# The lower part of the mixed filters, subtracted by VectorE in place of GpSimd

## The reference, cut to what matters

```python
x = x + attention(_gn(x))          # 1x1 projections, softmax of q over channels, of k over pixels, RMS norms
g = _gn(x)
r = sigmoid(relu(fc @ relu(rconv @ pooled(g)) + fc_b))   # (b, 3, c_in): a gate for each expert and input channel
w = einsum('bkc,kocij->bocij', r, expert_weight)         # filters of each image, 3 x 3 x 128 x 128
x = x + conv3x3(g, w)                                    # padding 1, stride 1
```

## Time and profile before

| | us |
|---|---|
| median of 3 runs (426.83 to 427.61) | 427.45 |
| the profiled execution | 427.47 |
| its span, first to last instruction | 425.8 |

### The profile page before, as it was taken

One profiled execution on the slowest core, in us unless ns is written; L12 is line 12 of the kernel. 1 busy time (PEld: TensorE's weight loads), 2 busy tenths in 40 slices (PEclk: granted clock), 3 DMA queues, 4 the chain that ended last, 5 costly groups with the idle time before them and its releaser, 6 DMA issues.

```text
span 425.8 us, 8949 instructions
## 1 busy us (share of the span) xinstructions
PE 410.8 (96%) x2575; PEld 360.0 (85%) x2575; DVE 345.7 (81%) x779; ACT 304.2 (71%) x942; POOL 265.7 (62%) x212
## 2 busy tenths in 40 slices
PE   7999989999999999999999999999999999999996
PEld 6889888879897888889898989889898989787785
DVE  4377989898988989897989899898989796978720
ACT  1688877888696777868686877879686868654321
POOL 4745859585774858577684848485876857543220
PEclk9899999999999999999999999999999999999999
DMA  6520261425324262606262444426062623405232
GB/s 202 231 101 2 99 237 62 180 84 187 147 98 153 96 248 94 240 36 228 100 247 100 165 179 145 200 75 239 35 242 99 247 100 117 181 12 237 99 149 99
DMA packets 19076, 61.63 MB, mean 145 GB/s; under 512 B 3024, under 2 KB 4320, under 8 KB 19040
## 3 DMA queue, kind: packets, MB, share of 16 engines
q1 hardware_dynamic: 19040, 61.21, 38.1%
HBM read 19.29 MB, written 8.39 MB: 65 GB/s over the span
## 4 chain that ended last, share of the span: by engine, by line
PE 54%; DVE 19%; issue 12%; ACT 10%; POOL 2%; DMA 1%; DVEq 1%; ACTq 0%; POOLq 0%
PE ps_conv L2176 19%; PE ps_y L2108 6%; PE ps_att L2076 6%; ACT y_scaled L820 4%; ACT expert_raw L847 4%; PE ps_y L2114 3%; DVE w_full L1523 3%; PE ps_y L2098 3%; PE ps_qkv L2057 3%; DVE y_scaled L1409 3%; PE ps_qkv L2059 2%; PE ps_qkv L2058 2%; DVE q_max L1337 2%; PE ps_att L2090 1%; DVE w_second L1516 1%
## 5 line engine op out<-in xcount | busy, mean ns | idle before, releaser
L2176 PE MATMUL ps_conv<-left,w_hi 128*128 128x512 f32 (+2 forms) x192 | 63.4, 398 | 0.0
L2176 PE MATMUL ps_conv<-right,w_hi 128*128 128x512 f32 (+2 forms) x192 | 62.9, 391 | 0.0
L761 ACT ACTIVATE qk<-ps_qkv,scale 128x256 f32<-128x256 f32 x128 | 54.7, 469 | 10.7 <-PE ps_qkv L2059 6.6
L589 POOL TENSOR_TENSOR w_lo<-w_full,w_hi 128x1152 fp32r<-128x1152 f32 x16 | 54.5, 3404 | 6.1 <-ACT w_hi L853 4.5
L596 POOL TENSOR_TENSOR left<-zeros 128x64 fp32r<-128x64 f32 x16 | 5.0, 313 | 77.9 <-DMA right<-img_lo 77.9
L570 POOL TENSOR_TENSOR scale<-ssq,minus_half 128x8 f32<-128x8 f32 x16 | 31.1, 1941 | 20.9 <-DVE ssq L1402 20.9
L544 POOL TENSOR_TENSOR x_lo<-x,x_hi 128x1024 fp32r<-128x1024 f32 x16 | 38.6, 2414 | 5.5 <-ACT x_hi L751 5.5
L2057 PE MATMUL ps_qkv<-wqk_hi,x_hi 128*128 128x256 f32 x128 | 40.5, 317 | 1.2 <-ACT qk L761 1.2
L2176 PEld LDWEIGHTS ps_conv<-right,w_hi 128*128 128x128 f32 x192 | 36.1, 188 | 5.9
L853 ACT ACTIVATE w_hi<-w_full 128x1152 fp32r<-128x1152 f32 x16 | 18.7, 1168 | 30.3 <-DVE w_full L1529 30.1
L2176 PEld LDWEIGHTS ps_conv<-left,w_hi 128*128 128x128 f32 x192 | 35.4, 189 | 5.0
(11 more groups left out here) (166 smaller groups left out, 1240.0 us busy)
## 6 DMA issues: line engine op xcount, KB each, us to landing
xa<-in_x_dram SPq DMA_DIRECT2D x16, 512.0 KB, 3.8
xb<-in_x_dram SPq DMA_DIRECT2D x16, 512.0 KB, 4.6
left<-img_hi SPq DMA_DIRECT2D x16, 511.5 KB, 2.9
right<-img_hi SPq DMA_DIRECT2D x16, 511.5 KB, 3.7
left<-img_lo SPq DMA_DIRECT2D x16, 511.5 KB, 2.9
right<-img_lo SPq DMA_DIRECT2D x16, 511.5 KB, 3.7
out_dram<-expert_raw SPq DMA_DIRECT2D x15, 512.0 KB, 3.0
expert_raw<-_conv_expert_weight_dram SPq DMA_DIRECT2D x1, 1728.0 KB, 9.4
```

The costliest lines, as they stand in the source:

```text
L589: nc.gpsimd.tensor_tensor(w_lo[p][:, :, :].rearrange("p t o -> p (t o)"), w_full[:, :], w_hi[p][:, :, :].bitcast(F32).rearrange("p t o -> ...
L761: nc.scalar.activation(qk[:, t, :], ps_qkv[t % 2][:, 0:QK], ACT.Copy, scale=scale1[:, t:t + 1]).then_inc(qkv_done, 1)
L2176: last = mm(into, weight[:, tap, :], pixels[:, top + down:bottom + down, :], start=(n == 0 and part == 0), stop=(n == TAPS - 1 and part == 2))
```

## The change

`filters_low` leaves GpSimd's list and joins VectorE's, with the same operands, the same waits and the same semaphore. In the loop it stands right behind `q_subtract`, on the filters that the step before has summed. In the lists by hand it stands behind `q_subtract` too, for images 0 to 13. That of image 14 stands behind `gn2_aggregate(15)`, and that of image 15 at the very end. On SyncE the last two calls are exchanged: the store of image 14 comes ahead of the store of image 15.

```diff
@@ sync, last_steps
                 store(13, 1)
+                store(14, 0)
                 store(15, 1)
-                store(14, 0)
@@ gpsimd
-            def filters_low(b, p):
-                pool.wait_ge(w_full_done, b + 1)
-                ...
@@ gpsimd, step (and likewise in first_steps and last_steps, for every image)
                 do(image_edges, t, p, 5)
-                do(filters_low, t, p, 5)
                 do(low1, t, p, 2)
@@ vector
+            def filters_low(b, p):
+                dve.wait_ge(w_full_done, b + 1)
+                dve.wait_ge(w_hi_done, b + 1)
+                if past(b, 2):
+                    dve.wait_ge(conv_ps, 2 * (b - 1))
+                v.tensor_tensor(w_lo[p][:, :, :].rearrange("p t o -> p (t o)"), w_full[:, :],
+                                        w_hi[p][:, :, :].bitcast(F32).rearrange("p t o -> p (t o)"),
+                                        ALU.subtract).then_inc(w_lo_done, 1)
@@ vector, step
                 do(q_subtract, t, p, 2)
+                do(filters_low, t, p, 4)
                 do(k_maximum, t, p, 2)
@@ vector, first_steps
                 q_subtract(2, 0)
+                filters_low(0, 0)
                 k_maximum(2, 0)
...
                 q_subtract(4, 0)
+                filters_low(2, 0)
                 k_maximum_all(4, 0)
@@ vector, last_steps
                 q_subtract(15, 1)
+                filters_low(13, 1)
                 k_maximum(15, 1)
...
                 gn2_aggregate(15, 1)
+                filters_low(14, 0)
                 gn2_pool(15, 1)
...
                 filters_centre(15, 1)
+                filters_low(15, 1)
```

More of the change, by code:

```diff
@@ L639, in first_steps @@
                 image_edges(0, 0)
-                filters_low(0, 0)
                 low1(3, 1)
@@ L650, in first_steps @@
                 image_edges(1, 1)
-                filters_low(1, 1)
                 low1(4, 0)
@@ L661, in first_steps @@
                 rms2(3, 1)
-                filters_low(2, 0)
                 low1(5, 1)
@@ L672, in first_steps @@
                 rms2(4, 0)
-                filters_low(3, 1)
                 low1(6, 0)
@@ L685, in last_steps @@
                 image_edges(11, 1)
-                filters_low(11, 1)
                 low1(14, 0)
@@ L696, in last_steps @@
                 image_edges(12, 0)
-                filters_low(12, 0)
                 low1(15, 1)
@@ L705, in last_steps @@
                 image_edges(13, 1)
-                filters_low(13, 1)
                 q_normalise(15, 1)
@@ L711, in last_steps @@
                 image_edges(14, 0)
-                filters_low(14, 0)
                 routing_products(15, 1)
@@ L715, in last_steps @@
                 image_edges(15, 1)
-                filters_low(15, 1)
             first_steps()
@@ L1707, in first_steps @@
                 q_subtract(3, 1)
+                filters_low(1, 1)
                 k_maximum(3, 1)
@@ L1787, in first_steps @@
                 q_subtract(5, 1)
+                filters_low(3, 1)
                 k_maximum(5, 1)
@@ L1829, in last_steps @@
                 q_subtract(13, 1)
+                filters_low(11, 1)
                 k_maximum(13, 1)
@@ L1867, in last_steps @@
                 q_subtract(14, 0)
+                filters_low(12, 0)
                 k_maximum(14, 0)
```

## The result

The changed kernel takes 465.52 us (median of 3 runs, 462.4 to 467.03), against 427.45 before. The ratio is 1.0883, with an interval of 1.0843 to 1.0922. The forecast was 444.6 us, in a range of 438.5 to 448.5: the sign was right and the size was not. The time grew by 38.1 us, and I had counted 17.1. The profiled execution took 465.52 us with a span of 463.8 us, so the traces differ by 38.0 us. One run of experiment e9 (452.4 us) was in a slower state of the chip and is left out of its row; all other times are of fast runs.

A forecast was written before the change was run, and what follows sets the result against it. TensorE was taken as the bound, with 0.06 us of slack per step. Steps 16.2, tail +2.4 and stores -1.5 summed to 17.1 us on 427.5, giving 444.6 us, in a range of 438.5 to 448.5.

The forecast's parts named there:

- The subtraction leaves GpSimd: On GpSimd, x_lo and q's normalisation can come up to 3.5 us earlier; counted as nothing.
- rival C: VectorE's other instructions shorten without a busy GpSimd, or part of the shift is caught up: 439.2 us, chance 0.12.
- The exception: Fourteenth filter's step, where y_scaled waited 1.09 us for GpSimd's scale and the convolution for w_lo: -0.2 us.
- The subtraction's time: Moved subtraction on VectorE: 1.36 us long, blocking the queue for 1.28 us, bounds 1.14 and 1.42.
- The step without the hold: Each loop step grows by 1.28 us to 24.7, as TensorE waits at L2070 and L2114; 16.2 us over all steps.
- The tail: Image 14's filters, behind image 15's aggregation on VectorE, come late; TensorE stands for 2.7 us: +2.4 us.
- The stores: At the end, image 14's store goes out earlier, ahead of image 15's: -1.5 us, between -0.4 and -1.7.
- Rival B: Not slower: VectorE's idle time swallows the subtraction and steps cost nothing; 428.2 us, chance 0.05.
- Rival D: Dearer steps: TensorE's pauses lower its granted clock, or the subtraction costs over 1.42 us; about 451 us, chance 0.08.
- The quoted rule on engine selection: Two-input elementwise work belongs on VectorE, GpSimd being about two times slower; set against 3.50 and 1.36 us.

The follow-up runs named there:

- e9: e8 without the wait that holds x_lo on GpSimd until q_exp is done; 445.5 us.
- e1: The changed kernel with one more wait on GpSimd: x_lo starts only when w_lo on VectorE is done; 447.0 us.
- e2: The kernel before with low1 (x_lo) moved ahead of filters_low in GpSimd's list, nothing else; 483.9 us.
- e4: The kernel before with the last two stores on SyncE exchanged, nothing else; 425.3 us.
- e8: Changed kernel, w_lo's products last, subtractions 0 to 13 ahead of gn1_stats, 14 behind y_scaled(15), x_lo waiting for q_exp; 430.2 us.

## Why the prediction was wrong, and where it was right

**The step that failed** is the first one, "The subtraction leaves GpSimd": "Both can now come up to 3.5 us earlier. I count nothing for that: the chain of the step goes through neither". What was put at nothing measured 18.5 us (465.5 against e1's 447.0). The chain doesn't go through x_lo in the kernel before, that is true. But x_lo moved from a place where none of VectorE's instructions is held to the start of k_max_part and q_exp. Its old place, timelines of GpSimd and VectorE, kernel before:

```profile
233.84 2.40 POOL L544 TENSOR_TENSOR x_lo<-x,x_hi 128x1024 fp32r<-128x1024 f32 x1
...
234.02 1.21 DVE L1352 TENSOR_REDUCE q_sum<-q_exp 128x32 f32<-128x1024 f32 x1
...
235.56 1.28 DVE L1421 SCALAR_TENSOR_TENSOR x<-ps_y,g_c,xb 128x1024 f32<-128x1024 f32 x1
```

The subtraction on GpSimd had been a shield. It waited behind q_exp itself (part of its 3.50 us, where an idle VectorE leaves 2.69), and it kept x_lo away until q_exp was over. e1 makes x_lo wait again and gives 447.0. e2 takes the shield away with nothing moved to VectorE and costs 56 us, with q_exp held too.

**The reading behind it** failed in rival C: "the contention falls on GpSimd alone". I took it from w_second, 1.42 us beside GpSimd's idle time and 1.42 at 224.98. But at 224.98 GpSimd was idle as well: it ran nothing between 224.36 and 229.03. A comparison of two undisturbed cases showed nothing. The trace of before held the counterexample, in the one step where the order slipped. VectorE and GpSimd, kernel before:

```profile
134.09 0.35 DVE L1308 TENSOR_TENSOR k_max_part<-k_quarter 128x128 f32<-128x128 f32 x1
134.37 1.31 DVE L1344 TENSOR_TENSOR q_exp<-qk,q_max 128x1024 f32<-128x1024 f32 x1
...
134.00 0.31 POOL L596 TENSOR_TENSOR left<-zeros 128x64 fp32r<-128x64 f32 x1 [7.95 <-DMA right<-img_lo]
134.25 0.36 POOL L597 TENSOR_TENSOR right<-zeros 128x64 fp32r<-128x64 f32 x1
134.56 2.62 POOL L570 TENSOR_TENSOR scale<-ssq,minus_half 128x8 f32<-128x8 f32 x1
```

k_max_part 0.35 and q_exp 1.31 us, against 0.28 or 0.29 and 1.21 to 1.23 in all other steps: small, because the edges that GpSimd was running had 64 columns and took 0.31 us. Behind a reader of 2.40 us it could be 2 us, an estimate from these rows. The scale behind them was held in its turn, 2.62 in place of 1.64 us. Read so, the rows give mechanism and size: up to 2 us in each step in which x_lo comes ahead of k_max_part.

**The exception** was wrong by sign: the step of y_scaled(4) was to become 0.2 us shorter, and became 1.6 longer. The same hold acts from the other side here. VectorE and GpSimd after:

```profile
143.28 0.28 DVE L1289 TENSOR_TENSOR k_max_part<-k_quarter 128x128 f32<-128x128 f32 x1
143.48 1.22 DVE L1325 TENSOR_TENSOR q_exp<-qk,q_max 128x1024 f32<-128x1024 f32 x1
144.62 1.35 DVE L1511 TENSOR_TENSOR w_lo<-w_full,w_hi 128x1152 fp32r<-128x1152 f32 x1
...
148.00 1.22 DVE L1390 TENSOR_TENSOR y_scaled<-ps_y,scale 128x1024 f32<-128x1024 f32 x1 [1.58 <-POOL scale L570]
...
143.27 2.86 POOL L587 TENSOR_TENSOR left<-zeros 128x64 fp32r<-128x64 f32 x1 [8.04 <-DMA right<-img_lo]
```

The edges on GpSimd, 0.31 us of work, came beside three instructions of VectorE with two inputs and ended at 146.13, just behind the last of them. So the engines don't take strict turns: VectorE's three went through back to back, each in its own time, although the edges' start is recorded 0.01 us ahead of the first. The scale, queued behind them, was late, and y_scaled waited 1.58 us for it.

**Right, by the runs.** The subtraction's time: forecast 1.36, measured 1.36, and 1.27 us between the starts of w_lo and of k_max (305.29 to 306.56), forecast 1.28. The step without the hold: forecast 24.7, measured 24.6 in e1 and 24.55 here. The tail: forecast a wait of 2.7 and +2.4, measured 2.37 at convolution 14 and a tail 0.5 us longer (35.5 against 35.03 from y_scaled(15)), for a forecast of 2.4 - 1.5. Against e4, which has the stores alone, the tail is 1.8 us longer. The stores: -1.5 forecast, -1.4 to -2.0 measured.

**Rival B**, that VectorE's idle time swallows the work, was rightly small at this place. e8 shows what was true in it: elsewhere in the list the same work costs 0.68 us a step in place of 1.2, and that much only with route_zr held. **Rival D** was small but real: the clock fell to about half in three windows of together 10 us. By the steps compared above that cost about 3 us (an estimate).

The quoted rule on engine selection (the Trainium skill, GPSIMD Engine Reference, Engine selection) gives the engine's time rightly. The fair pair is 1.36 against 2.69 us, twice as long; the 3.50 that I set against it has a hold in it. The rule says nothing about the place. The Trainium skill's Key points on the same page have the contention; I read them as a gain for VectorE only.

## What to carry to other kernels

When work leaves an engine, list what moves up in its queue and lay each such instruction beside the other engine's timeline at its new time, also where the chain passes through neither. For VectorE and GpSimd this means every pair of a two-input instruction on VectorE and a reader on GpSimd, since one of the two can wait for the whole of the other. Place work by the waits of its engine and not by its busy share: the same 1.27 us cost 1.2 us a step ahead of y_scaled, 1.1 behind it, and 0.7 where VectorE waits for a transfer, with a small instruction held in that 0.7.

## What the hardware showed that I had not expected

The hold is whole, not a slowdown: 0.28 us became 2.15 beside a 2.35 us reader, and q_exp became 3.67 in e2. It falls on either engine: GpSimd's rstd of 2 columns took 1.81 us in place of 0.70 in e8 where VectorE's w_lo was ahead of it.

It caught instructions with one tensor as input too. route_zr (0.86 against 0.17 us) and gate_n (0.79 against 0.23) scale three columns and were held beside GpSimd's x, while a reduction with one input ran through beside x_lo in 0.42 us. The Trainium skill (SBUF — State Buffer, Who interferes with whom) names such scalings as instructions that can enter a mode using the shared ports, and reductions as none. The runs agree with it on both, though no run here varied the operands to show that it is the mode.

TensorE's clock fell from 2.4 to 1.2 GHz (granted clock 0.50) for about 3 us at 69 us, behind two pauses of 2.10 and 1.39 us, and again behind pauses of 1.23 and 1.86 (at 96) and of 1.19 and 1.65 (at 174). In the step shown above, with pauses of 1.67, 0.73 and 0.37 us, it stayed at 1.00. It stayed there too from 380 to 400 us, around pauses of 1.25 and 1.65, so the length of the pauses alone doesn't tell the cases apart.
